# A 16-head attention stage: where TensorE waits for a free PSUM bank, and in which order the next trip's rows are measured

## The chip, the cores and the metric

The kernel runs on one NeuronCore of a Trainium2 chip. The metric is the device time of one execution in microseconds (us); of the kernel before there are three timed runs. Five engines work side by side, each in its own program order, and tell each other of finished work by counting semaphores: TensorE (PE in the profile, its weight loads are PEld), VectorE (DVE), ScalarE (ACT), GpSimd (POOL) and SyncE (SP, which here only starts DMAs). Products of TensorE land in PSUM, which has eight banks of 128 rows by 512 fp32 numbers.

## The reference, cut to what matters

The program is a chain of four residual blocks on an activation of 8 x 512 x 256 in fp32: an attention with one head of 256, a mixture of eight experts, a causal attention with 16 heads, and two layers of local attention. The change lies in the third:

```python
B, T, D, H = (2, 512, 256, 16)        # b is 8 at run time
DH = D // H                            # 16
qkv = x @ Wqkv.T                       # x is the layer-normed activation
q, k, v = ...                          # 16 heads of 16, q and k rotated by position
scores = jnp.einsum('bhqd,bhkd->bhqk', q, k) / math.sqrt(DH)
scores = jnp.where(causal, scores, -jnp.inf)
attn = jax.nn.softmax(scores, axis=-1)
out = jnp.einsum('bhqk,bhkd->bhqd', attn, v)
return out.transpose(0, 2, 1, 3).reshape(b, t, d) @ Wo.T
```

## The kernel before

The third block is the function `phase_attn1`. A barrier over all engines stands before and behind it. It takes the eight rows of the batch in four trips (`pair` in the code, trips 0 to 3 here) of two rows each (`s` 0 and 1, `NS = 2`). Each engine's program is written out by hand as a fixed list; nothing is planned by a scheduler.

A trip has four parts:

- **Projection.** `project`, `project_v` and `flip_qk` make q, k and v of both rows and lay q and k out with the head's numbers on the partitions.
- **The loop over chunks.** The 16 heads of both rows are worked off in eight chunks of two heads a row. Each chunk has six units `u` and six pieces `j`; piece `j` comes `SCORE_LAG` = 11 units behind unit `u`. At step `u` TensorE issues `scores(u)` (line 1301: queries by keys, for the maxima only), at every sixth step `flip_maxima` (line 1310), then `scores_turned(u - 11)` (line 1327: the scores again, keys by queries, with the maxima subtracted by two extra rows of q), and at every second step one of the three parts of `output` (line 1342: probabilities by v, and the row sums).
- **The end of the trip.** `raw_out` (ACT, line 1221), transposes, the division by the row sums (DVE `outputs`), the output projection and the residual, then the transposes of the next trip's rows.
- **The next trip's rows.** DVE's `first_norm(pair + 1)` stands behind the last `row_max` of the loop; it adds up the rows (`whole_rows`), measures them (`row_measure`, mean and variance) and normalises them (`row_norm`). Between measure and norm stands a power on POOL, `power_first` (line 957), for row 0 and then for row 1.

Who waits for whom in the loop:

- `scores(u)` writes one of four banks for each row. `free_place` (lines 1279 to 1287) waits until the user four places back is done: the maximum that DVE takes of it (`row_max`, line 1114), or ACT's copy of the turned maxima. The turned maxima take one of these places a chunk, behind the scores of its third unit.
- `scores_turned(j)` writes one of three banks. The product for row 0 needs the exponential of piece j-2, row 1, to be done, the one for row 1 the exponential of piece j-1, row 0 (ACT `exps`, line 1217; `m = NS * j + s - 3`). At a chunk's first piece it also waits for `nmax_rows` of both rows (line 1317): the maxima must have come back into q by DMA. Their way is `row_max` (DVE), `split_maxima` (POOL), `flip_maxima` (PE), `maxima_out` (ACT, line 1209), four DMAs by SP (line 939).
- Both functions wait for both rows first and then issue both rows' products. Row 0 and row 1 always take different halves of TensorE's 128 rows (`r = 64 * (h % 2)`, and `head` gives the two rows heads of different parity).
- `output(c, part)` needs the causal cut of the probabilities by POOL (`ban_keys`, line 1006), which needs the exponentials; its first part also needs the bank of the chunk before to be copied out (`raw_ready`). Output (7, 0) stands behind piece 45, (7, 1) behind piece 47, (7, 2) behind the end.
- POOL's list has `power_first(0)` and `power_first(1)` of the next trip, one behind the other, between the cuts of piece 41 and those of piece 43.

## Time and profile before

| | |
|---|---|
| median of three runs | 2533.52 us (2532.68 to 2536.14) |
| the profiled execution | 2531.52 us |
| its span, first to last instruction | 2529.8 us |
| mean granted TensorE clock | 0.939 |
| PE busy | 2267.8 us, 90% |
| DVE busy | 1555.9 us, 62% |
| ACT busy | 1315.7 us, 52% |
| POOL busy | 922.6 us, 36% |

The third block lies between about 600 and 1205 us of the span, so each trip takes about 150 us. "Busy" on PE is from modelled ends of pipelined products. The granted clock is a share of full speed, 2.4 GHz; it has two levels, 1.0 and 0.5 (1.2 GHz). An idle time in brackets is that of the engine just before the row's work, with the work that ended it as far as the semaphores tell. Instructions that only wait are called EVENT_SEMAPHORE; they belong to an engine's sequencer and are not busy time.

### The profile page before, as it was taken

What the parts mean: (1) busy time and instruction counts of PE and PEld (TensorE: products, weight loads), DVE (VectorE), ACT (ScalarE), POOL (GpSimd) and SP (SyncE); (2) the same over time, 40 slices, a digit from 0 to 9 for tenths busy, and PEclk for the clock granted to TensorE, in tenths of its full rate; (3) what the DMA queues carried; (4) which work ended last, traced back from release to release, by engine and by line L of the source; (5) the groups of instructions that cost most, each with busy time, mean ns of one, the idle gap of its engine ahead of it and who ended that gap; (6) DMA issues with size and microseconds to landing.
All of it is one profiled execution on the core that took longest, in us unless ns stands there. A gap on an engine that the chain in (4) does not pass through costs nothing.

```text
span 2529.8 us, 45343 instructions
## 1 busy us (share of the span) xinstructions
PE 2267.8 (90%) x15874; PEld 1748.3 (69%) x15874; DVE 1555.9 (62%) x4796; ACT 1315.7 (52%) x3214; POOL 922.6 (36%) x1363
## 2 busy tenths in 40 slices
PE   7999599996778788877699999999999999999998
PEld 5777499994445363544567777777777777777777
DVE  6665422224666757565667676777777667776675
ACT  2221133333555755465555675666755675656753
POOL 2221122213434433332543344333544445343451
PEclk9999699998787988878899999999999999999999
DMA  3222411112001010100200000000101000000000
GB/s 132 100 100 90 130 36 37 39 30 79 19 10 59 3 59 11 35 35 11 88 9 18 16 3 18 18 18 10 44 26 62 19 9 26 26 26 18 10 18 26
DMA packets 75937, 96.41 MB, mean 38 GB/s; under 512 B 6113, under 2 KB 69090, under 8 KB 75458
## 3 DMA queue, kind: packets, MB, share of 16 engines
q1 hardware_dynamic: 70786, 81.89, 9.7%
q0 software_dynamic: 3408, 9.31, 1.3%
q8 instruction: 131, 2.15, 0.4%
q10 hardware_dynamic: 1520, 2.31, 0.3%
q14 instruction: 92, 0.75, 0.1%
HBM read 62.69 MB, written 30.28 MB: 37 GB/s over the span
## 4 chain that ended last, share of the span: by engine, by line
PE 27%; DVE 9%; ACT 8%; issue 5%; POOL 3%; DMA 0%; SPq 0%; DVEq 0%; POOLq 0%; ACTq 0%
PE l_free L2194 4%; PE l_free L2196 4%; PE l_free L2195 3%; PE l_out L2309 3%; PE l_score L2269 2%; POOL l_probs L1684 2%; PE l_turned L2290 2%; DVE l_probsT L1779 2%; DVE l_work L1856 2%; PE l_turned L2194 1%; PE l_turned L2196 1%; PE l_turned L2195 1%; DVE l_u_low L1862 1%; ACT l_probs L2068 1%; PE l_turned L2243 1%
## 5 line engine op out<-in xcount | busy, mean ns | idle before, releaser
L1684 POOL TENSOR_SCALAR l_probs<-l_probs,l_rinv 128x256 f32<-128x256 f32 (+1 forms) x512 | 223.5, 456 | 227.6 <-DVE l_rinv L1839 227.5
L1114 DVE CUSTOM_DVE_ANT_0 c_raw<-cbank,c_later 128x256 f32<-128x256 f32 (+3 forms) x512 | 218.3, 487 | 73.3 <-PE cbank L1301 73.0
L2068 ACT ACTIVATE l_probs<-l_probs,l_nmax 128x256 f32<-128x256 f32 (+1 forms) x512 | 239.9, 473 | 26.5 <-DVE l_nmax L1834 26.4
L1217 ACT ACTIVATE c_cprobsT<-cbank 128x384 f32<-128x384 f32 (+1 forms) x384 | 180.9, 525 | 95.8 <-PE cbank L1327 95.7
L1834 DVE CUSTOM_DVE_ANT_0 l_probs<-l_score,mask,l_inv 128x256 f32<-128x256 f32 (+1 forms) x512 | 200.0, 447 | 28.8 <-PE l_score L2269 28.1
L2194 PE MATMUL l_free<-l_part,l_w_high 128*128 128x512 f32 x384 | 166.4, 433 | 9.6 <-DVE l_probsT L1779 6.6
L2194 PE MATMUL l_free<-l_wqkv_high,l_yT 128*128 128x512 f32 x384 | 159.0, 414 | 1.9 <-DVE l_part L1758 1.9
L1817 DVE COPY l_probsT<-l_turned 128x512 f32<-128x512 f32 (+1 forms) x128 | 79.9, 624 | 131.3 <-PE l_turned L2290 80.3
L1006 POOL TENSOR_SCALAR_AFFINE_SELECT c_cprobsT<-c_cprobsT 128x256 f32<-128x256 f32 x256 | 99.6, 413 | 154.3 <-ACT c_cprobsT L1217 152.2
L2196 PE MATMUL l_free<-l_part,l_w_low 128*128 128x512 f32 x384 | 153.0, 398 | 0.0
L2195 PE MATMUL l_free<-l_yT,l_w_high 128*128 128x512 f32 x384 | 152.8, 398 | 0.0
L2195 PE MATMUL l_free<-l_wqkv_low,l_yT 128*128 128x512 f32 x384 | 152.2, 396 | 0.0
L2196 PE MATMUL l_free<-l_wqkv_high,l_part 128*128 128x512 f32 x384 | 152.0, 396 | 0.0
L760 PE MATMUL h_bank<-m_xsT,m_w1s 128*128 128x128 f32 x1248 | 148.3, 278 | 0.4 <-issue 0.4
L760 PEld LDWEIGHTS h_bank<-m_xsT,m_w1s 128*128 128x128 f32 x1248 | 145.0, 195 | 0.8 <-issue 0.7
L685 POOL DMA_INDIRECT m_xs<-xn_d,source x39 | 62.8, 1610 | 218.4 <-PE xT_bank L748 182.9
L2269 PE MATMUL l_score<-l_kT,l_flipped 64*128 64x256 f32 (+1 forms) x1024 | 129.5, 371 | 13.3 <-DVE l_nmax L1834 13.3
L769 PE MATMUL y_bank<-w,m_hT 128*128 x624 | 141.0, 379 | 0.0
L704 DVE TENSOR_TENSOR m_y<-y_bank,b 128x256 f32<-128x256 f32 x39 | 16.6, 425 | 200.0 <-PE y_bank L769 200.0
L2309 PE MATMUL l_out<-l_probsT,l_v 128*64 128x128 f32 x1792 | 128.1, 283 | 12.6 <-ACT l_oT L2086 12.6
L1327 PE MATMUL cbank<-c_cqT,c_ckT 64*128 64x256 f32 (+2 forms) x512 | 96.4, 409 | 46.8 <-ACT c_cprobsT L1217 39.6
L735 ACT ACTIVATE m_hT<-h_bank,m_b1s 128x128 f32<-128x128 f32 x312 | 89.2, 368 | 84.7 <-PE h_bank L760 75.8
(282 smaller groups left out, 5932.1 us busy)
## 6 DMA issues: line engine op xcount, KB each, us to landing
w<-in_W1T SPq DMA_DIRECT2D x8, 1024.0 KB, 8.0
w<-in_W2T SPq DMA_DIRECT2D x8, 1024.0 KB, 11.8
ys_d<-m_y SPq DMA_DIRECT2D x39, 128.0 KB, 1.7
xn_d<-a_prods SPq DMA_DIRECT2D x8, 512.0 KB, 3.6
c_came<-x_d SPq DMA_DIRECT2D x8, 512.0 KB, 4.9
y_d<-c_raw SPq DMA_DIRECT2D x8, 512.0 KB, 3.7
early_rows<-y_d SPq DMA_DIRECT2D x8, 512.0 KB, 3.7
l_came<-y_d SPq DMA_DIRECT2D x8, 512.0 KB, 3.9
```

Source lines behind the costliest of these rows:

```text
L760: last = pe.matmul(h_bank[2 * (j % 2) + h][:, f, :], w1s[j % 2][:, c, (4 * h + f) * P:(4 * h + f + 1) * P], xsT[:, j % 2, c, :], start=c = ...
L769: last = pe.matmul(y_bank[j % 2][:, 0:D], hT[:, j % 2, f, :], w, start=f == 0, stop=f == FC - 1)
L1114: last = dve.tensor_tensor_reduce(raw[:, CHUNKS - NS + s, h * 2 * P:h * 2 * P + wide], score_place("scores", u, s)[:, h * 2 * P:h * 2 * P ...
L1217: act.activation(probsT[s][:, c % 2, i, k0:k0 + w], turned_place(j, s)[:, 0:w], ACT.Exp).then_inc(probs_ready[s], 1)
L1684: pool.tensor_scalar(a, a, rinv[:, j, r, h:h + 1], 1.0, ALU.mult, ALU.mult).then_inc(normed, 1)
L1834: dve.tensor_tensor_reduce(probs[:, j % 2, r, h, 0:width], score_bank[r][:, 2 * P * h:2 * P * h + width], ban, inv[s][:, w, head:head + 1] ...
L2068: act.activation(a, a, ACT.Exp, bias=nmax[:, j, r, h:h + 1], scale=-1.0, accum_out=rsum[:, j % 2, r, h:h + 1])\
L2194: pe.matmul(out, a[0], b[0], start=start, stop=False)
L2195: pe.matmul(out, a[0], b[1], start=False, stop=False)
L2196: return pe.matmul(out, a[1], b[0], start=False, stop=stop)
L2269: last = pe.matmul(score_bank[half][:, 2 * P * h:2 * P * h + width * P], qT[s][r, p, w * P:(w + 1) * P], kT[s][r, p, k0 * P:(k0 + width) * ...
L2309: last = pe.matmul(out_bank[DH2 * half:DH2 * (half + 1), at:at + P], v[s][:, k0 + k, head:head + DH2], probsT[:, j % 2, half, 2 * h + k, : ...
```

## The change

Four edits in `phase_attn1`:

- In `first_norm`, for trips 1 to 3, `row_measure(1)` is issued before `row_norm(0)`. For trip 0 the order stays.
- In `scores`, the wait for a free place is issued for each row just ahead of that row's first product, no longer for both rows ahead of both. The waits of the first unit (`u == 0`) stay ahead of both.
- In `scores_turned`, the wait for the free bank is moved in the same way. The waits for `nmax_rows` stay ahead of both.
- In the loop over steps, output (7, 0), the first part of the last chunk's outputs, is issued behind piece 46 in place of piece 45.

```diff
-                        row_norm(0)
-                        row_measure(1)
+                        if trip:
+                            row_measure(1)
+                            row_norm(0)
+                        else:
+                            row_norm(0)
+                            row_measure(1)
                         row_norm(1)
...
-                        for s in range(NS):
-                            if u == 0:
+                        if u == 0:
+                            for s in range(NS):
                                 pe.wait_ge(qkT_ready[s], pair * (4 * NT) + 4 * NT)
                                 pe.wait_ge(v_ready[s], pair * NT + NT)
-                            free_place("scores", u, s)
                         wide = max(2, qt + 1) * P
                         for i in range(n):
                             for s in range(NS):
+                                if i == 0:
+                                    free_place("scores", u, s)
...
-                        for s in range(NS):
-                            if j % PER_CHUNK == 0:
+                        if j % PER_CHUNK == 0:
+                            for s in range(NS):
                                 pe.wait_ge(nmax_rows[c % 2][s], pair * (16 * CHUNKS) + 32 * (c // 2 + 1))
-                            m = NS * j + s - 3
-                            if m >= 0:
-                                pe.wait_ge(probs_ready[m % NS], pair * UNITS + m // NS + 1)
                         for kt in kts:
...
                             for s in range(NS):
+                                m = NS * j + s - 3
+                                if kt == kts[0] and m >= 0:
+                                    pe.wait_ge(probs_ready[m % NS], pair * UNITS + m // NS + 1)
...
                         for part in range(3):
-                            if j >= 3 and (j - 3 - 2 * part) % PER_CHUNK == 0 and 0 <= j - 3 - 2 * part < UNITS:
+                            if part == 0 and u == UNITS + SCORE_LAG - 3:
+                                continue
+                            if part == 0 and u == UNITS + SCORE_LAG - 2:
+                                output(CHUNKS - 1, part)
+                            elif j >= 3 and (j - 3 - 2 * part) % PER_CHUNK == 0 and 0 <= j - 3 - 2 * part < UNITS:
                                 output((j - 3 - 2 * part) // PER_CHUNK, part)
```

## Rows read from the trace of the kernel before

**Rows 1.** TensorE's timeline, a chunk of trip 3: start us, length, what [idle before].

```profile
1148.55 0.42 PE L1310 MATMUL cbank<-c_identr,c_nmax_hl 128*32 128x128 f32 x4 [0.44 <-DVE c_cnmax L1114]
...
1153.35 0.49 PE L1327 MATMUL cbank<-c_cqT,c_ckT 64*128 64x512 f32 x2
...
1154.60 0.51 PE L1327 MATMUL cbank<-c_cqT,c_ckT 64*128 64x512 f32 x2 [0.52 <-ACT c_cprobsT L1217]
...
1155.82 0.51 PE L1301 MATMUL cbank<-c_ckT,c_cqT 64*128 64x512 f32 x2
...
1157.11 0.30 PE L1310 MATMUL cbank<-c_identr,c_nmax_hl 128*32 128x128 f32 x2 [0.43 <-DVE c_cnmax L1114]
```

**Rows 2.** Timelines of SP, ACT and DVE in the same chunk.

```profile
1149.61 2.38 SPq L939 DMA_DIRECT2D c_cqT<-c_nmaxT  x4
...
1153.85 1.08 ACT L1217 ACTIVATE c_cprobsT<-cbank 128x512 f32<-128x512 f32 x2 [0.86 <-PE cbank L1327]
...
1156.35 0.69 DVE L1114 CUSTOM_DVE_ANT_0 c_raw<-cbank,c_later 128x512 f32<-128x512 f32 x1 [0.83 <-PE cbank L1301]
```

**Rows 3.** Single lines: instructions, duration ns min/median/max, first and last start; whole trace, then windows.

```profile
L1320 PEldq EVENT_SEMAPHORE  x184: 51/51/51, 666.4 to 1177.8; - x184
...
L1336 PEldq EVENT_SEMAPHORE  x28: 51/51/3101, 677.6 to 1174.0; - x28
...
L1317 PEldq EVENT_SEMAPHORE  x1: 51/51/51, 1153.1 to 1153.1; - x1
...
L1320 PEldq EVENT_SEMAPHORE  x1: 51/51/51, 1154.5 to 1154.5; - x1
...
L1327 PE MATMUL cbank<-c_cqT,c_ckT x2: 473/488/502, 1154.6 to 1154.6; 64*128 64x512 f32 x2
```

**Rows 4.** Timelines of ACT and TensorE in trip 1's first chunk with pieces.

```profile
814.43 1.09 ACT L1217 ACTIVATE c_cprobsT<-cbank 128x512 f32<-128x512 f32 x2 [0.39 <-PE cbank L1327]
...
815.17 0.69 PE L1327 MATMUL cbank<-c_cqT,c_ckT 64*128 64x384 f32 x2 [0.35 <-ACT c_cprobsT L1217]
```

**Rows 5.** POOL's timeline at the end of trip 1's loop.

```profile
873.51 1.05 POOL L957 TENSOR_TENSOR c_crstd<-c_cve,minus_half 128x4 f32<-128x4 f32 x1
878.00 1.01 POOL L957 TENSOR_TENSOR c_crstd<-c_cve,minus_half 128x4 f32<-128x4 f32 x1 [3.44 <-DVE c_cve L71]
878.98 1.64 POOL L1006 TENSOR_SCALAR_AFFINE_SELECT c_cprobsT<-c_cprobsT 128x256 f32<-128x256 f32 x4
```

**Rows 6.** TensorE's timeline there.

```profile
877.63 0.69 PE L1327 MATMUL cbank<-c_cqT,c_ckT 64*128 64x384 f32 x2 [0.67 <-ACT c_cprobsT L1217]
879.90 1.94 PE L1342 MATMUL cbank<-c_cprobsT,c_cv 128*32 128x512 f32 x8 [1.57 <-POOL c_cprobsT L1006]
881.76 0.80 PE L1327 MATMUL cbank<-c_cqT,c_ckT 64*128 64x256 f32 x4
883.23 0.80 PE L1327 MATMUL cbank<-c_cqT,c_ckT 64*128 64x256 f32 x4 [0.67 <-ACT c_cprobsT L1217]
883.95 1.51 PE L1342 MATMUL cbank<-c_cprobsT,c_cv 128*32 128x384 f32 x8
```

**Rows 7.** ACT's timeline there.

```profile
877.00 0.87 ACT L1217 ACTIVATE c_cprobsT<-cbank 128x384 f32<-128x384 f32 x2
878.33 0.87 ACT L1217 ACTIVATE c_cprobsT<-cbank 128x384 f32<-128x384 f32 x2 [0.46 <-PE cbank L1327]
```

**Rows 8.** TensorE's timelines: output (7, 0) of trips 0 and 2, pieces of trip 3.

```profile
731.72 1.93 PE L1342 MATMUL cbank<-c_cprobsT,c_cv 128*32 128x512 f32 x8 [2.73 <-POOL c_cprobsT L1006]
...
1029.37 1.93 PE L1342 MATMUL cbank<-c_cprobsT,c_cv 128*32 128x512 f32 x8 [1.74 <-POOL c_cprobsT L1006]
...
1174.00 0.69 PE L1327 MATMUL cbank<-c_cqT,c_ckT 64*128 64x384 f32 x2 [0.92 <-ACT c_cprobsT L1217]
...
1177.95 0.80 PE L1327 MATMUL cbank<-c_cqT,c_ckT 64*128 64x256 f32 x4 [0.67 <-ACT c_cprobsT L1217]
```

**Rows 9.** Busy us (instructions) of PE, PEld, DVE, ACT, POOL; granted clock, DMA share, GB/s.

```profile
876.00:889.00 13.00, 8.62 (x55) 3.31 (x48) 3.57 (x13) 4.68 (x10) 4.10 (x9) 0.50 0.00 0
```

## The prediction
> **What bounds the kernel now.** I read the timeline of TensorE in the chunk loop first, then those of the engines that end its waits, then the end of a trip. Only `phase_attn1` is touched, and barriers enclose it, so a microsecond saved on its path is one saved in the end.
>
> In the steady loop a chunk takes 8.56 us, from one `flip_maxima` (1148.55) to the next (1157.11) [rows 1]; the trace has five such periods in each of the four trips, 8.53 to 8.57. No engine is full there. One chain closes on itself. The flip at 1148.55 feeds ACT's copy and SP's four DMAs, which begin at 1149.61 [rows 2]. TensorE's sequencer gets past the wait for the landed maxima at 1153.1 [rows 3] and issues the first piece at 1153.35 [rows 1]. ACT begins its exponential at 1153.85, after 0.86 idle [rows 2]; the next piece waits for it, with 0.52 of idle before 1154.60. Then stand an output part and the scores at 1155.82 [rows 1]. DVE has been idle 0.83 when it takes their maximum at 1156.35 [rows 2], and the next flip waits 0.43 for that [rows 1]. Every link waits for the one before it or stands right behind it on TensorE, so what shortens a link shortens the period.
>
> At the end of a trip the chain is another. POOL does the power for row 0 at 873.51, then sits 3.44 until DVE has normalised row 0 and measured row 1, does the second power at 878.00, and only at 878.98 comes to the causal cut [rows 5]. Output (7, 0) needs that cut: TensorE stands 1.57 before 879.90 [rows 6]. Piece 46 is behind it in TensorE's order, though its bank has long been free. The same stall is 2.73 in trip 0 and 1.74 in trip 2; trip 3 has no next trip, and there output (7, 0) did not wait for the cut [rows 8].
>
> **Edit 1, both waits moved to their products.** It removes no wait, but it changes what each wait holds and how it is issued.
>
> How it is issued: a TensorE instruction carries one wait in the trace, further ones are instructions of the sequencer. There are 184 at line 1320 [rows 3] and 156 at line 1285. Output part 0 of chunks 1 to 7 has three waits in the code and one such instruction each, 28 in all [rows 3], so two waits fit into one. After the edit row 0's load carries row 0's wait and row 1's load row 1's, and nearly all of the 340 go. The price of one on the path: it starts at 1154.5 and the product at 1154.60 [rows 3, 1], so at most 0.10, of which 0.051 is its own length. I take 0.08. The steady chain has two. The first stands before 1154.60. The other is at a chunk's first piece, where four waits (two landed maxima, two banks) now take two instructions between 1153.1 and 1153.35 [rows 3, 1], and the three left ahead of row 0's product take one. That makes 0.16, bounds 0.05 to 0.20 a chunk. Five periods by four trips by 0.16 is **3.2 us**.
>
> What it holds: the two rows' products of a piece run at the same time. The pair at 1154.60 is over in 0.51 and each single product lasts 0.473 to 0.502 [rows 3, 1]. So row 0's product alone, put into idle time, takes nothing off TensorE's work behind the wait: row 1's still needs a whole pass. It helps ACT, which gets row 0 before it has run dry. In the steady chunk that is worth nothing, since the chain there goes through row 1's product. It does help where pieces follow each other closely at the slow clock. In trip 1's first chunk with pieces ACT idled 0.39 before 814.43, and piece 2 started at 815.17 only after that exponential (0.35 idle) [rows 4]. With row 0 in time, ACT starts 0.39 earlier and the piece goes as soon as TensorE is through with the scores before it. The piece's own idle bounds this at 0.35. I add 0.1 for the waits of the two pieces after it and 0.1 for the second product ahead of the first flip: 0.55 for the start of a trip, bounds 0.1 and 0.8. Four trips: **2.2 us**. Between the last flip and the end of the loop the saved instructions of three more pieces count, 0.2 a trip: **0.8 us**.
>
> Where TensorE has a backlog, the sequencer is ahead of it and the waits are hidden in both versions: zero. Every product starts at the earliest when its own conditions hold and no later than before, and the consumers' orders are fixed, so I see no place where the waiting itself makes anything later.
>
> The Trainium skill (Perfetto Trace Analysis, Identifying Dependency Chains) says that an instruction with more waits may get EventSemaphore instructions ahead of it; the trace agrees with its 184 and 156. The page gives no price. At zero a piece the term of 3.2 would be nothing, and that result is the first rival.
>
> **Edits 2 and 3, the end of a trip.** With `row_measure(1)` ahead of `row_norm(0)`, DVE has both variances before POOL comes to the powers at 873.51: DVE has then been idle since it added row 1 up, over 3 us, and a norm and a measure together fit into POOL's 3.44. So the powers follow each other, 873.51 to about 875.6 [rows 5], and the cut of piece 43 waits for its exponential alone, which is over before ACT begins piece 44's at 877.00 [rows 7]. Two cuts of 0.41 (a quarter of 1.64 [rows 5]) are done by 877.8, before TensorE, at piece 45 from 877.63 on, reaches output (7, 0) in either place. Cost: row 0's norm comes no later, since it waits for the power, and row 1's comes earlier.
>
> What is late next, in the order of edit 3: piece 45 at 877.63, its exponential from 878.33, 0.44 for row 0 (half of 0.87) [rows 7], so piece 46 at 878.8 in place of 881.76. Behind it output (7, 0): piece 47 was followed by its output after 0.72 (883.23 to 883.95), and output (7, 0) was followed by the next piece after 1.86 [rows 6]. Piece 47 then goes at 878.8 + 0.72 + 1.86 = 881.4 in place of 883.23: **1.8 us** in trip 1. From piece 47 on (its exponentials, the cut of the last keys, output (7, 2), the copy) the chain is as before. Edit 1 adds here: ACT idles 0.46 before 878.33 with row 0's bank free [rows 7], so up to 0.5 more; I take 0.4, so 2.2. The 1.8 is the stall of 1.57 and 0.25; with its stall of 1.74 trip 2 gives 2.0 + 0.4 = 2.4. Trip 0, with 2.73, gives 3.0, and up to 0.9 more (half of 1.86) if output (7, 0), which ran at the slow clock there (1.93) [rows 8], now falls into the fast one; I take 3.8 in all. In trip 3 there was no stall. Piece 47 still stands behind output (7, 0): 1174.00 + 0.70 (877.63 to 878.33) + 0.44 + 0.72 + 1.86 = 1177.7 for 1177.95 [rows 8], 0.2, and 0.3 for ACT. Together 2.2 + 2.4 + 3.8 + 0.5 = **8.9 us**, bounds 7.0 (no help from edit 1) and 10.5.
>
> Edit 3 alone is worth little beside edit 2: whichever of piece 46 and output (7, 0) goes first, piece 47 waits for both, and the gain is the wait for one exponential hidden under the output, 0.3 a trip; it is in the sums above. Without edit 2 it would let piece 46 go under the stall.
>
> **Sum.** 3.2 + 2.2 + 0.8 + 8.9 = 15.1 us. The profiled execution took 2531.5 us with its 1.7 around the span, so it would take 2516.4. The median of the runs lies 2.0 above it: **2518.4 us**.
>
> The granted clock is the part that I can't work out. The end of trip 1's loop ran at 0.50, 1.2 GHz, throughout, though PE was busy for 8.62 of 13.00 us there [rows 9]; output (7, 0) took 1.94 in it [rows 6]. Moved work meets the change of level elsewhere. If one such output a trip changes level either way, 0.9 each, that is 3 to 4 us over the kernel; I put 3 us on both sides for it.
>
> **Rivals.**
> 1. *The waits' instructions cost nothing.* A wait carried by a load could take as long to be seen as one of its own, or the chain could go by the path over the fifth piece's output and not over the DMAs. For it: the profile calls the idle before a load "issue" rather than a wait. Against: the product follows that instruction by 0.10 each time. Then 3.2 and most of 0.8 and 2.2 are missing, 9 to 10 us remain: 2524.
> 2. *The end's gain is given back.* POOL's stall goes but the clock takes it: a wrong phase at four trips' ends, or piece 47 behind output (7, 0) at the slow clock in trip 0. Then the loop's 6 us and some 2 to 3 of the end remain: 2525.
> 3. *Pairs come apart.* With a wait between them, row 1's product could start late even where both banks are free, and a pair would take two passes. For it: the two now start together, behind all waits. Against: the sequencer is ahead wherever TensorE has work waiting. It costs a pair between nothing and the 0.50 that a product lasts. There are 384 pairs with a moved wait (12 a chunk), so it decides from 15.1 / 384 = 0.04 us on each; at 0.06, about what one sequencer's instruction takes, it costs 23 us: 2541, slower.
> 4. *No change.* All that is saved is met by the clock: 2533.
>
> The Trainium skill (TensorE: Matmul & The Clock Gate, Part 3) has matmuls on different row groups run at once but start and end in program order. By it a late row 1 also holds what stands behind it. The trace agrees with the overlap, 0.51 for two; what a wait between the two does, no row shows.
>
> **How the numbers follow.** Forecast 2518.4 with 0.64 (its own range 2513 to 2524), rival 1 with 0.17, rival 2 with 0.10, rival 3 with 0.05, rival 4 with 0.04. The range is 2511 to 2527: below by the upper bounds of the terms (19) and 3 of clock, above over rivals 1 and 2. About 0.2% (5 us) is what a measurement of this kernel tells from no change. Faster by more: 0.91; within: 0.05; slower by more: 0.04.
>
> **What would show it.** Steps at lines 1285 and 1320 all but gone from the sequencer's instructions; steady periods of 8.35 to 8.45 us between flips; POOL's two powers within 2.1 us; output (7, 0) without a wait for POOL, behind piece 46; the last output part 2 to 4 us nearer to piece 45 in trips 0 to 2. Wrong would be: periods of 8.55 as before (rival 1), pairs that start more than 0.05 apart where TensorE has no idle (rival 3), a longer time at 0.50 (rivals 2 and 4).

## The result

2501.98 us in the median (2500.28 to 2507.50, four runs) against 2533.93 for the kernel before on the same chip; the ratio is 0.9874, 95% interval 0.9857 to 0.9891. That is 32 us gained where 15.1 were forecast, and below the range. The two profiled executions lie 24.0 us of span apart (2529.8 to 2505.8); the profiled one was the slowest of the four, with 0.944 for the mean granted clock against 0.950 and 0.951 in the other three.

### The profile page after: what moved, and what is told of

It reads as the page before. It is cut to its first block, busy times and chain, and to the rows that moved or that the text cites. A ratio compares the mean times of both kernels' runs of the same rounds, so it can differ in the third digit from the quotient of the medians.

```text
span 2505.8 us, 44975 instructions
## 1 busy us (share of the span) xinstructions
PE 2285.2 (91%) x15874; PEld 1764.6 (70%) x15874; DVE 1553.9 (62%) x4796; ACT 1313.2 (52%) x3214; POOL 921.1 (37%) x1363
## 4 chain that ended last, share of the span: by engine, by line
PE 27%; DVE 9%; ACT 8%; issue 5%; POOL 3%; DMA 0%; SPq 0%; DVEq 0%; POOLq 0%; ACTq 0%
PE l_free L2203 4%; PE l_free L2205 4%; PE l_free L2204 3%; PE l_out L2318 3%; PE l_score L2278 2%; POOL l_probs L1693 2%; PE l_turned L2299 2%; DVE l_probsT L1788 2%; DVE l_work L1865 2%; PE l_turned L2203 1%; PE l_turned L2205 1%; PE l_turned L2204 1%; DVE l_u_low L1871 1%; ACT l_probs L2077 1%; PE l_turned L2252 1%
## 5 line engine op out<-in xcount | busy, mean ns | idle before, releaser
L1332 PE MATMUL cbank<-c_cqT,c_ckT 64*128 64x256 f32 (+2 forms) x512 | 117.0, 396 | 25.8 <-ACT c_cprobsT L1221 16.5
```

## The profile after

TensorE's timeline of the chunk in trip 3 that answers to [rows 1]. The piece behind the first, `x2` at 1154.60 before, is now one product for row 0 at 1123.94 and one for row 1 at 1124.55:

```profile
1118.75 0.42 PE L1315 MATMUL cbank<-c_identr,c_nmax_hl 128*32 128x128 f32 x4 [0.43 <-DVE c_cnmax L1118]
...
1123.40 0.50 PE L1332 MATMUL cbank<-c_cqT,c_ckT 64*128 64x512 f32 x2
...
1123.94 0.39 PE L1332 MATMUL cbank<-c_cqT,c_ckT 64*128 64x512 f32 x1
1124.55 0.50 PE L1332 MATMUL cbank<-c_cqT,c_ckT 64*128 64x512 f32 x1 [0.22 <-ACT c_cprobsT L1221]
...
1125.77 0.50 PE L1306 MATMUL cbank<-c_ckT,c_cqT 64*128 64x512 f32 x2
...
1127.06 0.41 PE L1315 MATMUL cbank<-c_identr,c_nmax_hl 128*32 128x128 f32 x4 [0.43 <-DVE c_cnmax L1118]
```

From flip to flip it is 8.31, before 8.56. The first piece stands 4.65 behind its flip (before 4.80), the next 1.15 behind it (before 1.25), and from there on every distance is as it was.

The sequencer's instructions that carry a wait, by line; count, duration min/median/max in ns:

```profile
L1329 PEldq EVENT_SEMAPHORE  x28: 51/1248/1512, 675.2 to 1146.3; - x28
L1339 PEldq EVENT_SEMAPHORE  x68: 51/51/51, 670.1 to 1158.7; - x68
L1341 PEldq EVENT_SEMAPHORE  x28: 51/51/51, 680.0 to 1153.3; - x28
```

Those for the turned scores' banks fell from 184 [rows 3] to 28, one at a chunk's first piece, where the landed maxima are waited for as well; in `scores` 156 went and none is left. Those of the outputs (L1341 is L1336 of before) stayed at 28.

The end of trip 1's loop on POOL and on TensorE, for [rows 5, 6]:

```profile
866.55 2.18 POOL L957 TENSOR_TENSOR c_crstd<-c_cve,minus_half 128x4 f32<-128x4 f32 x2
868.58 0.81 POOL L1006 TENSOR_SCALAR_AFFINE_SELECT c_cprobsT<-c_cprobsT 128x256 f32<-128x256 f32 x2
```

```profile
868.42 0.87 PE L1332 MATMUL cbank<-c_cqT,c_ckT 64*128 64x384 f32 x3
869.59 1.56 PE L1332 MATMUL cbank<-c_cqT,c_ckT 64*128 64x384 f32 x5 [0.30 <-ACT c_cprobsT L1221]
871.08 1.93 PE L1347 MATMUL cbank<-c_cprobsT,c_cv 128*32 128x512 f32 x8
872.94 0.80 PE L1332 MATMUL cbank<-c_cqT,c_ckT 64*128 64x256 f32 x4
873.67 1.51 PE L1347 MATMUL cbank<-c_cprobsT,c_cv 128*32 128x384 f32 x8
875.96 1.51 PE L1347 MATMUL cbank<-c_cprobsT,c_cv 128*32 128x256 f32 x16 [0.78 <-POOL c_cprobsT L1006]
```

The two powers follow each other without the 3.44 between them, the cut comes right behind them, and output (7, 0) at 871.08 waits for nobody, behind piece 46. The steps that were forecast happened. But compare the four ends. Windows from the last flip to the last output part, trips 0 to 3; columns: length, busy us of PE, PEld, DVE, ACT, POOL, the granted clock, DMA:

```profile
720.40:734.10 13.70, 10.21 (x84) 4.21 (x83) 7.43 (x26) 10.00 (x23) 8.36 (x18) 1.00 0.01 2
860.90:876.00 15.10, 12.45 (x84) 4.94 (x85) 7.35 (x26) 10.03 (x23) 8.29 (x18) 0.76 0.01 2
1003.60:1017.30 13.70, 10.22 (x84) 4.22 (x84) 7.39 (x26) 9.98 (x23) 8.29 (x18) 1.00 0.01 2
1142.70:1158.90 16.20, 13.59 (x84) 5.35 (x85) 0.00 (x0) 10.25 (x23) 5.71 (x15) 0.68 0.01 2
```

The same 84 products take 13.7 us where the clock was 1.00 throughout and 15.1 or 16.2 where it had a part at 0.50. In the kernel before none of the four ends kept its fast clock.

To place the gain I cut every profiled execution at the same instructions, and added up its four trips. *Start* is from the first scores to the third flip, *chunks* from there to the eighth and last flip, *tail* from there to the last output part, *end* from there to the first `wo` product, *half* the time of the tail at a granted clock of 0.50. Us:

```
kernel                                          start  chunks    tail     end    half
before                                          114.0   167.3    72.5    44.6    39.1
changed, first profile                          108.7   162.2    58.4    43.0    17.3
changed, again (all_again)                      107.4   162.2    54.5    43.2     0.0
edit 1 (waits_only)                             109.1   162.3    68.0    45.2    22.2
its half at first scores (waits_scores)         113.5   167.3    73.3    44.4    43.5
its half at turned scores (waits_turned)        107.4   162.3    70.7    44.3    37.1
edit 2 (measure_only)                           113.2   167.3    68.4    44.4    43.1
edit 3 (output_only)                            115.7   167.4    69.0    41.2    37.2
edits 2, 3 (tails_only)                         118.6   167.3    68.4    38.9    41.3
edits 1, 3 (waits_output)                       109.2   162.2    65.9    43.7    25.0
edits 1, 2 (no_output)                          109.2   162.3    57.5    45.0    11.5
one wait, row 0 held (one_wait_held)            112.7   162.4    69.9    44.2    23.1
row 0 free, both waits (row0_free_two_waits)    113.2   163.5    69.0    44.9    24.0
one wait held, edits 2, 3 (held_tails)          113.0   162.4    61.1    43.0    20.9
edit 2, added products (measure_fill)           116.5   167.2    61.1    39.0     0.0
all, added in the tail (all_fill_tail)          108.5   162.3    58.2    40.0     0.0
all, added at the start (all_fill_start)        107.7   162.2    60.3    44.6    28.9
all, and trip 0's order (all_trip0)             110.6   162.2    61.3    45.7    28.2
```

The first two rows give 5.3 + 5.1 + 14.1 + 1.6 = 26.1 us. Outside the cuts the profiled execution lost some 2: the untouched stretch ahead of the loop was 3.8 us longer. The second profile gives 6.6 + 5.1 + 18.0 + 1.4 = 31.1 us. Its 2499.46 us and granted clock of 0.950 are those of most timed executions, so it is the better guide.

## The experiments

Ratios are to the kernel before on the same chip, with 95% intervals; gains in us are (1 - ratio) times 2533. The intervals reach 2.4 to 4.7 us to each side.

**The three edits one by one, and together again.** Each kernel is the one before with only the named hunks of the diff.

`waits_only`, edit 1:

```diff
-                            free_place("scores", u, s)
+                                if i == 0:
+                                    free_place("scores", u, s)
...
+                                if kt == kts[0] and m >= 0:
+                                    pe.wait_ge(probs_ready[m % NS], pair * UNITS + m // NS + 1)
```

> The change's first edit alone: each wait at its product, the tails as before. The changed kernel gained 32 us where 15.1 were forecast. Theory A (the waits were mis-sized): in the trace of the changed kernel the steady period fell by 0.25 us in place of 0.16, and the stretch from the first scores to the third flip by 1.36, 0.66, 1.49 and 1.80 us; four steady periods by four trips, one shorter period by four, and those starts make 4.0 + 1.1 + 5.3 = 10.4 us, and a microsecond or two at the ends: 2521 to 2524. Theory B (the forecast's size, and the excess lies in the ends): 6.2 us, 2527 to 2528. Periods of 8.28 to 8.32 under A; 8.35 to 8.45 under B.

0.9949 (0.9935 to 0.9963), 12.9 us; periods of 8.28 to 8.33. Theory A, with more than its 10.4.

`measure_only`, edit 2:

```diff
-                        row_norm(0)
-                        row_measure(1)
+                            row_measure(1)
+                            row_norm(0)
```

> The second edit alone: on later trips both rows are measured before row 0 is normalised. Theory A (the tails add up as the forecast's steps say, with the third edit worth 0.3 a trip): 6 to 9 us, 2525 to 2528; POOL's two powers within 2.2 us, output (7, 0) without a wait for the causal cut in trips 0 to 2, trip 3 unchanged. Theory B (the clock is the larger part: a shorter stall keeps TensorE at the fast level at the trip's end): 12 us and more, below 2522, with the stretch at 0.50 behind the last flip of trips 0 and 2 cut from 13.7 and 17.1 us to some 3.

0.9974 (0.9964 to 0.9984), 6.6 us, with the tail at 17.10 or 17.11 in all four trips. Theory A by size; and the clock did not stay up: 43.1 us at half speed. Trip 3, which was to stay unchanged, took 0.9 us more (17.11 for 16.20), with 10.8 us at 0.50 for 6.9.

`output_only`, edit 3:

```diff
+                            if part == 0 and u == UNITS + SCORE_LAG - 3:
+                                continue
+                            if part == 0 and u == UNITS + SCORE_LAG - 2:
+                                output(CHUNKS - 1, part)
```

> The third edit alone: output (7, 0) one piece later, DVE's order as before. Piece 46 can go under POOL's stall of 3.44 us, but the output still waits for the cut and piece 47 stands behind it. Theory A (as forecast): piece 46 no longer stands behind the output, and one exponential (0.44) is hidden in each trip, up to the 0.7 that the piece takes: 1 to 3 us, 2530 to 2533, within measurement of no change. Theory B (the order is a large part of the gain, since ACT gets piece 46 2 to 3 us earlier and the tail of the pipeline follows it): 5 us and more, 2528 or less.

0.9975 (0.9966 to 0.9985), 6.3 us: theory B. Alone it was worth as much as the reordered measuring.

`all_again`, the changed kernel unchanged:

> The changed kernel once more, beside its parts on the same chip: 2500 to 2504. If the three parts alone sum to 28 to 36 us they are independent; if they sum to under 24, one of the edits only pays beside another (theory B of the others: the third edit beside the second, or the clock, which stays up only when both stalls are gone).

0.9870 (0.9854 to 0.9886), 32.9 us. The parts sum to 25.8, which lies between the two limits that were set (28 and 24). Some 7 us belong to no edit alone, but the four intervals together (the root of their squares' sum, 6.4 us) are nearly as large. The pairs below are clearer: edit 1 alone and the other two together give 12.9 + 9.1 = 22.0, so 10.9 are missing there.

**The pairs, and edit 1 by halves.** `no_output` has edits 1 and 2, `tails_only` 2 and 3, `waits_output` 1 and 3, `waits_turned` edit 1 in `scores_turned` alone; each is the sum of hunks shown above.

> The first and second edits together, output (7, 0) in its old place. Alone they took 12.9 and 6.6 us off (ratios 0.9949 and 0.9974), the third alone 6.3, all three 33. Theory A (the first two add, and the third is worth its 6 us anywhere, since it puts piece 46 ahead of a long output part): 2533 - 19.5 = 2514. Theory B (the surplus of 7 us lies between the waits and the measuring): 2507 or less. Theory C (the surplus needs the third edit: only with piece 46 early does TensorE stay busy enough to keep its fast clock to the last output): 2514 or more, with 13 us and more at 0.50 behind the last flip of each trip, against 3.4 in the kernel with all three.

0.9906 (0.9892 to 0.9919), 23.8 us: more than A's 19.5, at the edge of B. Two of its four tails ran at full clock, and two had 5.7 us at half speed, less than C wanted.

> The second and third edits together, the waits as before. Theory A (additive): 2533 - 12.9 = 2520. The forecast's own number for the two was 8.9 with 1.3 of it from the first edit: 2525 to 2526. Theory C (the fast clock held at the end is the surplus and the two edits suffice for it): 2514 to 2516, with the last output part 13.6 to 14.5 us behind the last flip in all four trips and 3.4 us at 0.50 there.

0.9964 (0.9949 to 0.9979), 9.1 us. The forecast had 7.0 to 8.9 for the two, without and with edit 1's help, and the time came near it; theory A's 12.9 is the very edge of the interval. Its twelve executions, us and mean granted clock of each:

```
2513.58 0.948   2516.18 0.947   2519.16 0.945   2521.79 0.946
2525.98 0.941   2526.71 0.938   2526.93 0.937   2527.62 0.939
2527.75 0.938   2528.46 0.938   2529.99 0.938   2531.68 0.938
```

One program, 18 us apart, and the order is nearly that of the clock. The two shortest lie where theory C had all of them. The profiled execution (2527.62) was of the longer kind, so where the clock stayed up in the short ones no profile shows; and 9.1 is a mean over both kinds.

> The first and third edits together, DVE's order as before: POOL's stall of 3.4 us stays in trips 0 to 2. Theory A (additive): 2533 - 19.2 = 2514. Theory C: the stall before output (7, 0) is still there, so the clock falls there in trips 0 to 2 and the surplus is missing or shows in trip 3 alone: 2514 to 2518. If instead the time is near 2507, the surplus lies between these two edits and not with the measuring.

0.9929 (0.9916 to 0.9941), 18.0 us: here the two add.

> The first edit in the turned scores alone (their bank waits at their products); the first scores wait as before, for both rows ahead of both. The edit in both places took 12.9 us off. In the steady chunk the trace has 0.13 us saved ahead of the chunk's first piece and 0.09 ahead of the next one, both turned scores. Theory A (all of the gain is in the turned scores, the other 156 instructions stand where TensorE has a backlog): 2520 to 2522, steady periods 8.28 to 8.34. Theory B (both halves count, the scores' at the start of a trip where row 0's bank is free before row 1's): 2523 to 2527, with the stretch from the first scores to the first flip as in the kernel before and only the steady part shortened.

0.9947 (0.9935 to 0.9959), 13.4 us: theory A, all of edit 1's gain.

**The instruction or the freedom of row 0.** Row 0 is called free where its product may go before row 1's bank is. `one_wait_held` keeps both rows behind one wait, for the exponential that ends later:

```diff
-                            m = NS * j + s - 3
-                            if m >= 0:
-                                pe.wait_ge(probs_ready[m % NS], pair * UNITS + m // NS + 1)
+                        m = NS * j - 2
+                        if m >= 0:
+                            pe.wait_ge(probs_ready[m % NS], pair * UNITS + m // NS + 1)
```

> The kernel before, with one wait ahead of both rows of a turned piece in place of two: that for the younger exponential, which ACT does after the older one, so nothing is waited for less. It takes the extra instruction away and still holds row 0. The first edit in the turned scores took 13.4 us off. Theory A (the instruction is the price: 0.08 to 0.13 us on each of two links a chunk): the steady period falls from 8.55 to some 8.35 and the ends too; 2520 to 2526. Theory B (what counts is that row 0 is free to go, so that ACT always has a row ready and never idles between exponentials): little, 2529 to 2533, periods of 8.45 and more, and ACT still idles 0.15 to 0.5 us before each piece's exponentials behind the last flip.

0.9951 (0.9937 to 0.9966), 12.4 us. Its chunk on TensorE, and `row0_free_two_waits` below it, whose edit is

```diff
+                                for m in range(NS * j - 3, NS * j + s - 2):
+                                    if kt == kts[0] and m >= 0:
+                                        pe.wait_ge(probs_ready[m % NS], pair * UNITS + m // NS + 1)
```

> The kernel before, with row 0's wait at its product and, ahead of row 1's product, both waits once more: row 0 is free to go, and the extra instruction of the sequencer stays, now ahead of row 1. Theory A (the instruction is the price): 2529 to 2533, periods of 8.5 and more. Theory B (row 0's freedom is the price): most of the 13.4 us, 2520 to 2524, ACT without idle between the exponentials behind the last flip; the steady period keeps part of the gain, 8.35 to 8.45, since the link through row 1 still has the instruction.

0.9956 (0.9942 to 0.9970), 11.1 us. TensorE's timeline in the first kernel, from the chunk's first piece to the next flip, and then the same in the second:

```profile
1150.10 0.50 PE L1327 MATMUL cbank<-c_cqT,c_ckT 64*128 64x512 f32 x2
...
1151.25 0.50 PE L1327 MATMUL cbank<-c_cqT,c_ckT 64*128 64x512 f32 x2 [0.42 <-ACT c_cprobsT L1217]
...
1153.76 0.42 PE L1310 MATMUL cbank<-c_identr,c_nmax_hl 128*32 128x128 f32 x4 [0.43 <-DVE c_cnmax L1114]
```

```profile
1149.57 0.60 PE L1327 MATMUL cbank<-c_cqT,c_ckT 64*128 64x512 f32 x2
...
1150.82 0.47 PE L1327 MATMUL cbank<-c_cqT,c_ckT 64*128 64x512 f32 x1 [0.29 <-ACT c_cprobsT L1217]
...
1153.29 0.42 PE L1310 MATMUL cbank<-c_identr,c_nmax_hl 128*32 128x128 f32 x4 [0.44 <-DVE c_cnmax L1114]
```

Their sequencers' instructions at the turned scores, the first kernel and the second:

```profile
L1320 PEldq EVENT_SEMAPHORE  x28: 51/547/787, 676.2 to 1165.6; - x28
```

```profile
L1324 PEldq EVENT_SEMAPHORE  x212: 51/51/1446, 667.3 to 1172.0; - x106
```

By time and period each kernel met the theory that it was meant to favour: the first kernel theory A, and the second theory B (periods of 8.34 to 8.39). The links say why. In the steady chunk theory A holds: with the instruction gone and row 0 held, the chunks take 162.4 us, those of the changed kernel 162.2. The second kernel tells the links apart. Ahead of the chunk's first piece it has one instruction fewer before row 0's product, and saves as much there (the flip was at 1144.92, so 4.65 behind it, for 4.80 before); ahead of the next piece the kept instruction stands before row 1's product, and that piece is 1.25 behind the first, as before, where the first kernel has 1.15. Its period is 8.35, between 8.55 and 8.30. Row 0's freedom adds nothing there.

At a trip's start it is otherwise: neither kernel alone shortens the sum much (112.7 and 113.2 for 114.0), and the half of edit 1 that does both brings it to 107.4. The sum hides what row 0's freedom does. From the first flip to the second, where ACT takes the first pieces, trips 1 to 3 took 8.86 to 8.89 before, 8.76 to 8.79 with row 0 held, 8.32 to 8.35 with row 0 free and the instruction kept, and 8.25 to 8.30 with both, so nearly all of it is the freedom. The first interval went the other way (10.1 us in three trips of each of these two kernels, 10.0 and 10.1 in two of the kernel before, 9.72 else and in `waits_turned`), and the third goes mostly by the clock, as shown below. And a good part of the 11 to 12 us of these two is clock: 23 and 24 us at half speed in the tail for 39, with trip 3's tail at 14.2 and 14.0 us for 16.2.

**What lies behind the last flip.** `held_tails` has edits 2 and 3 and the one held wait:

> The second and third edits with the single wait held ahead of both turned rows (the extra instruction gone, row 0 not free). With the full first edit the three took 33 us off; the second and third alone 9. The single held wait alone took 12.4 us. Theory A (the saved instruction gives the surplus, wherever it stands): as with all three, 2500 to 2504, the last output part 13.6 to 15.1 us behind the last flip. Theory B (behind the last flip it is row 0's freedom that keeps ACT, and through it TensorE, busy): the sum of the parts, 2510 to 2516, with the last part 16 to 17 us behind the flip and ACT idle 0.1 to 0.5 ahead of each piece's exponentials.

0.9939 (0.9925 to 0.9953), 15.5 us, less than the sum of its parts (21.5) and 17 short of the changed kernel. That refutes theory A. It is nearer to theory B, though both missed: its tails are 14.7 and 15.9 us, not 16 to 17, and the time lies just above B's. Against the second profile of the changed kernel 5.6 us of the shortfall are at the starts and 6.6 in the tails, where 20.9 us ran at half speed for none. ACT's timelines show what row 0's freedom does there. `measure_only` (both rows held, extra instruction), then `held_tails`, then the changed kernel again, each from the exponentials of piece 42 on; trip 3, trip 1 and trip 1:

```profile
1166.05 1.09 ACT L1221 ACTIVATE c_cprobsT<-cbank 128x512 f32<-128x512 f32 x2 [1.00 <-PE cbank L1331]
1167.59 1.08 ACT L1221 ACTIVATE c_cprobsT<-cbank 128x512 f32<-128x512 f32 x2 [0.46 <-PE cbank L1331]
1169.09 0.60 ACT L1225 ACTIVATE c_raw<-cbank 128x512 f32<-128x512 f32 x1 [0.41 <-PE cbank L1346]
1169.68 0.87 ACT L1221 ACTIVATE c_cprobsT<-cbank 128x384 f32<-128x384 f32 x2
1171.00 0.87 ACT L1221 ACTIVATE c_cprobsT<-cbank 128x384 f32<-128x384 f32 x2 [0.46 <-PE cbank L1331]
```

```profile
869.68 2.27 ACT L1221 ACTIVATE c_cprobsT<-cbank 128x512 f32<-128x512 f32 x4 [1.00 <-PE cbank L1331]
871.85 0.60 ACT L1225 ACTIVATE c_raw<-cbank 128x512 f32<-128x512 f32 x1
872.32 1.91 ACT L1221 ACTIVATE c_cprobsT<-cbank 128x384 f32<-128x384 f32 x4
874.44 0.87 ACT L1221 ACTIVATE c_cprobsT<-cbank 128x384 f32<-128x384 f32 x2 [0.21 <-PE cbank L1331]
```

```profile
860.33 2.06 ACT L1221 ACTIVATE c_cprobsT<-cbank 128x512 f32<-128x512 f32 x4 [1.14 <-PE cbank L1332]
862.33 0.60 ACT L1225 ACTIVATE c_raw<-cbank 128x512 f32<-128x512 f32 x1
862.83 2.60 ACT L1221 ACTIVATE c_cprobsT<-cbank 128x384 f32<-128x384 f32 x6
```

With row 0 free, ACT runs eleven instructions in 5.10 us without a pause (860.33 to 865.43). With both rows held they take 5.63, with pauses of 0.1 inside the runs and 0.21 at the end. In `measure_only` nine of them take 5.82, but from 1166.4 on at the slow clock; the other two ran wholly at the fast one. Row 0's product runs under the previous exponential, so ACT's chain no longer passes through a load and a product at every piece. In the tail no scores stand between, and ACT is what the pieces wait for. Trip 3 gives the price at equal clock, as three kernels without edits 2 and 3 ran its tail wholly at 1.00: 14.17 us with row 0 held (`one_wait_held`), 13.97 with row 0 free and the instruction kept (`row0_free_two_waits`), 13.76 with edit 1. Row 0's freedom is worth 0.4 us a trip beside the saved instruction. The rest of the shortfall in the tails has the form of the clock.

`waits_scores` is edit 1 in `scores` alone:

> The first edit in the first scores alone. In both places it took 12.9 us, in the turned scores alone 13.4. Theory A (the scores' waits stand where TensorE has a backlog, or where DVE's maximum sets the pace): 2531 to 2535, no change; steady periods 8.53 to 8.57. Theory B (row 0's scores early feed DVE at the start of a trip): the first flip 0.4 us nearer to the first scores in each trip, 1 to 2 us in all, 2530 to 2533.

1.0005 (0.9993 to 1.0017), no change: theory A. The first flip did come 0.4 to 0.7 us earlier in each trip (9.36 behind the first scores for 9.72 to 10.06), 2.0 us in all. In the profile the third intervals took 1.6 of it back, trip 0's with 11.46 us for 10.04, where the clock was back at 1.00 later.

**The clock.** `measure_fill` adds work to `measure_only`:

```diff
+                        if u >= UNITS + MAX_LAG - 1 and j < UNITS - 1:
...
+                            spare = score_bank[(rotation.index(("maxima", CHUNKS - 1, 0)) + 1) % 4]
+                            for _ in range(1):
+                                pe.matmul(spare[:], kT[0][:, 0, 0:P], qT[0][:, 0, :], start=True, stop=True)
```

> The kernel with the second edit alone, whose last output part stood 17.1 us behind the last flip in all four trips with 17.1 us of TensorE at 0.50 there, and with one idle-time product of 512 columns into an unused scores bank after each of the last nine pieces' output slots, whose result nobody reads. It adds work of about 0.43 us each. Theory A (the clock is the cause of the long tail): TensorE keeps its fast clock behind the last flip, and the tail falls to 14 to 15 us in spite of the added work: 8 to 12 us less than 2525.7, 2514 to 2518. Theory B (the tail is 17.1 us because of its chain through ACT and POOL, the clock follows from it): no gain, the added work costs 0 to 2 us a trip, 2526 to 2533.

0.9923 (0.9910 to 0.9937), 19.5 us: theory A, 12.9 us better than the kernel that it adds work to. By the profiles the tails fell by 7.3 us and the ends by 5.4, and the starts took 3.3 more. The tail of trip 3 without the products and with them:

```profile
1160.10:1177.30 17.20, 12.52 (x84) 4.63 (x86) 0.00 (x0) 10.43 (x24) 5.77 (x16) 0.68 0.01 2
```

```profile
1155.30:1170.60 15.30, 12.27 (x92) 5.08 (x94) 0.00 (x0) 10.26 (x23) 5.75 (x15) 1.00 0.00 1
```

Eight products more, 1.8 us less, and a granted clock of 1.00 (2.4 GHz) for 0.68, a mixture of that and 0.50 (1.2 GHz). TensorE had stood idle 0.6 to 0.75 us before most pieces, and with the products at most 0.35 was left. The Trainium skill (TensorE: Matmul & The Clock Gate, Part 1, HAM oscillation) tells of this gate falling while matmuls wait for a DMA and of the price that the next ones pay. The price is in this trace, with 17.2 and 15.3 us; the waits are others, mostly for ACT, and no idle time in the 10 us ahead of the fall was longer than 0.75.

`all_fill_tail` does the same to the changed kernel (that hunk in all three edits), `all_fill_start` fills idle time ahead of the first scores:

```diff
+                            n_fill = {(8, 1): 3, (9, 1): 3}.get((i, j), 0)
+                            if n_fill:
+                                pe.wait_ge(v_ready[0], pair * NT + NT)
+                            for _ in range(n_fill):
+                                pe.matmul(bank[0][1][:], xnT[0][:, 0, 0:P], xnT[0][:, 0, :], start=True, stop=True)
...
+                    for _ in range(1):
+                        pe.matmul(bank[0][1][:], xnT[0][:, 0, 0:P], xnT[0][:, 0, :], start=True, stop=True)
```

> The changed kernel with one idle-time product of 512 columns after each of the last nine pieces' slots, read by nobody, as the kernel with the second edit and such products, where the tail fell from 17.1 to 15.3 us and the time by 9 to 13 us. Theory A (the surplus of the changed kernel is this same clock, already held): little is left, 0 to 3 us either way, 2498 to 2503, the tail between 13.6 and 14.5 us in every trip and no trip at 15.1. Theory B (the clock still falls in many timed executions and the products hold it): 2492 to 2497. Theory C (the added products now stand in the way, since TensorE has less idle time there): 2504 to 2510.

0.9876 (0.9858 to 0.9894), 31.4 us: theory A. Where the clock is held already, the products cost 0.9 a tail (14.54 for 13.62), 3.7 in all. In the profile the ends behind them were 3.2 shorter, and in time nothing is gained.

> The changed kernel with all three edits, and seven idle-time products of 512 columns (0.485 us each by the projections' rows) where TensorE waits for the last flips of q and k: three, three and one, of 1.45, 1.67 and 0.89 us idle; nobody reads them. TensorE's clock falls there at each trip's start and stays at 0.50 for 24 to 27 us, in which the first 14 us of scores keep it busy. Theory A (the idle stretches bring the clock down, and the scores behind them are bound by it): 2 to 5 us less a trip, 2480 to 2492. Theory B (the clock falls anyway, or the scores there are bound by DVE's maxima, not by TensorE): 2500 as before, or up to 4 us more for the added work.

0.9898 (0.9882 to 0.9914), 25.8 us: 7 less than the changed kernel. Theory A is refuted, and the loss is larger than theory B's 4. The clock did fall later at the start (17.1 us at 0.50 for 23.9 and more), and the first flip came 0.3 nearer (9.06 to 9.10 for 9.36). But the first scores came 1.2 to 1.5 us later. The clock was back at 1.00 only 3.2 to 3.4 us behind the second flip, for 2.4 to 2.6 in the second profile of the changed kernel, and the third interval took 9.5 or 9.6 for 9.1 or 9.2. So the start took 107.7 for 107.4: an early stretch at the fast clock is worth 0.3 us there, and a late one is worth more. And the same instructions in the tail now met the slow clock, in all four trips. Trip 0's tail here, and that of the changed kernel:

```profile
720.40:735.50 15.10, 12.51 (x84) 5.00 (x86) 7.30 (x26) 10.00 (x23) 8.23 (x18) 0.76 0.01 2
```

```profile
714.70:728.40 13.70, 10.21 (x84) 4.25 (x86) 7.39 (x26) 9.97 (x23) 8.34 (x18) 1.00 0.01 2
```

`all_trip0` drops the `if trip:` and measures both rows first everywhere:

```diff
-                        if trip:
-                            row_measure(1)
-                            row_norm(0)
-                        else:
-                            row_norm(0)
-                            row_measure(1)
+                        row_measure(1)
+                        row_norm(0)
```

> The changed kernel with the measuring of both rows first on the first trip as well, for a version that may be faster. The first trip's rows are normalised before the chunk loop. Theory A (nobody waits there for the first row alone): 2500 to 2503, no change. Theory B (TensorE's first transposes of row 0 wait for that norm, which now comes one measuring later): 0.5 to 2 us more.

0.9906 (0.9888 to 0.9925), 23.8 us, 9 worse than the changed kernel: both theories missed. In its profile all four tails have a stretch at 0.50 (15.07, 16.10, 15.07 and 15.07 us), the last of them some 500 us behind the edit, and its five timed executions have a mean clock of 0.939 to 0.946. The loss has the form of the clock; why the slow stretches came to lie so is open. No version tried beats the changed kernel.

## Why the prediction was wrong in size

The step that failed is the clock: it was set down as 3 us of noise on both sides, beside terms that hold at one clock. The runs show it as the largest part of what is missing behind the last flip (18.0 us for 9.7), and as a part at the starts. The saved instruction and the freed row were the right causes, and their sizes were too small.

**Edit 1 in the steady chunks: right cause, price too small.** 3.2 us forecast, 5.1 measured (167.3 to 162.2). I had 0.08 us for each of two links; they measured 0.15 and 0.10, so the sum of 0.25 lies above my upper bound of 0.20. In the trace of before, the sequencer's instructions in a row start 0.11 apart, twice their own length of 0.051, and 0.08 was too near to the length. The count was nearly right: four periods of 8.53 to 8.57 fell by 0.25, and the fifth, which I had wrongly put in the same band, is 7.64 and fell by 0.27. That nearly all of the 340 instructions go (312 did) and that row 0 early is worth nothing there held; `one_wait_held` shows the second.

**Pairs did come apart.** Counted in the traces, none of the 512 pairs of `scores` and `scores_turned` products starts more than 0.05 us apart before, and 164 do in the changed kernel's first profile. At 99 of them TensorE had no idle time just before either product: the sign that was set down for rival 3. The two rows' products then run one behind the other. From the second scores of trip 0 on, the kernel before and then `waits_scores`:

```profile
650.82 0.69 PE L1301 MATMUL cbank<-c_ckT,c_cqT 64*128 64x384 f32 x2 [1.04 <-DVE c_cnmax L1114]
```

```profile
650.24 7.88 PE L1302 MATMUL cbank<-c_ckT,c_cqT 64*128 64x384 f32 x18 [0.33 <-DVE c_cnmax L1114]
```

Before, these 18 products stand with idle time between them and end 10.03 us behind the first scores; run without a pause, with the rows one behind the other, they end 9.43 behind them. Over the four trips TensorE is busy for 145.4 us of the chunks where it was for 140.3, and for 97.1 of the starts for 82.8, and yet the time fell: the places waited for are not free earlier, and row 0 uses the time until row 1's is. Whether a busier TensorE also has a part in which clock the tails get, no run separates. `one_wait_held`, in which no pair comes apart, kept the fast clock in one tail of four, as `waits_only` did.

**Edit 1 at a trip's start: mis-sized, and in part the clock.** 2.2 us forecast, 5.3 to 6.6 measured. I had taken the gain of one piece (0.35) and 0.1 for two more. But ACT's pauses went at every piece: in trip 1 of the changed kernel's second profile the first six exponentials are one run,

```profile
802.39 2.84 ACT L1221 ACTIVATE c_cprobsT<-cbank 128x512 f32<-128x512 f32 x6 [4.46 <-PE cbank L1332]
```

where before the second pair alone had 0.39 ahead of it [rows 4]. The first two intervals, both wholly at the slow clock, fell by 0.4 and 0.6 us in that trip (9.73 to 9.36, 8.86 to 8.26), the third by another 0.4. Over the four trips the three intervals give 2.0, 2.4 and 2.2 us in the second profile. The first of these, by `waits_scores`, brought nothing when it came alone. The third is not edit 1's alone. Over all the kernels it goes from 8.44 us, where the clock was back at 1.00 0.4 us behind the second flip (`waits_turned`, trip 1), to 11.46, where that was 8.5 us behind (`tails_only`, three trips). Where the clock is back at the same moment, edit 1 takes 0.1 to 0.2 off it: 9.33 to 9.13 at 2.4 us, 10.04 to 9.86 at 4.15. So some 1.5 us of the surplus at the starts are the clock's, an estimate from these rows.

**Behind the last flip: the step that failed.** For the end of the loop I had 0.8 for edit 1's instructions and 8.9 for edits 2 and 3 with its help, 9.7; the tails fell by 14.1 us in the first profile and 18.0 in the second. The ends, at which I had put nothing, gave 1.6 and 1.4 more. By trips, against the first profile: 2.4 forecast for trip 1, which kept a slow stretch, and 3.7 measured; 4.0 and 2.6 for trips 0 and 2, which ran wholly at the fast clock, and 5.1 each; 0.7 for trip 3, and 0.1, with 10.2 us at half speed for 6.9 before. So where only the kernel before had a slow stretch the gain was 1.1 and 2.5 us more than forecast. Where both had one, it was 1.3 more with that stretch shortened by 5.4 us (trip 1) and 0.6 less with it lengthened by 3.3 (trip 3). How much the whole of edit 1 is worth at equal clock no pair of runs shows cleanly, since no tail of the kernel before was wholly fast. An estimate: `measure_fill`, wholly at the fast clock, has tails of 15.3, its products cost 0.9 a tail where the clock was up anyway, and `no_output` has 13.75, so 0.6 or 0.7 a trip, about what was forecast. Yet timed, edit 1 took 17.2 us beside edit 2 (6.6 to 23.8) and 12.9 alone. I had priced it as time on a path. What it also does is keep ACT, and so TensorE, from pausing just where the clock is about to fall.

**Edits 2 and 3.** Between 7.0 and 8.9 us by themselves; 9.1 (5.3 to 12.9) measured. The steps for DVE, POOL and the order of TensorE were seen, but that the sum came out so near is luck. In the profile of `tails_only` the tails fell by 4.1 us, the ends, which I had at nothing, by 5.7, and the starts took 4.6 more: ends of 9.2 us at a clock of 1.00, and starts with the clock back late. Edit 3 beside edit 2 was put at 0.3 a trip. At equal clock it is 0.13 in tails wholly at 1.00 (13.75 to 13.62) and nothing in those with a stretch at 0.50 (15.0, 15.07), so the order itself is worth no more than I said; yet timed it took 9 us off (23.8 to 32.9). The profiles of `no_output` and `all_again` lie 7.2 us apart: 3.0 in the tails, of which four of four kept the fast clock for two of four, and 1.8 each at the starts and ends.

**The clock: 3 us on both sides was far too narrow, and not symmetric.** The part of the tails at half speed went from 39.1 us to 17.3 and, in the second profile, to none, and the tails from 72.5 to 58.4 and 54.5. A tail costs 1.4 us more with 7.2 us at 0.50 and 2.5 more with 10.2. I had treated the clock as noise that meets moved work; but an edit that takes idle time out of TensorE also decides which clock the rest gets. This is where most of the 7 us lie which no edit has alone: the tails fall by 4.5, 4.1 and 3.5 us in the three single kernels and by 18.0 in the kernel with all. Why a given trip falls on one side is not settled. In the two tails of the changed kernel's first profile in which it fell, it did so 8 and 6 us behind the last flip, behind the same instructions as in the two in which it did not.

**The rivals.** Rival 1 is refuted by `one_wait_held`. Rival 3's sign was seen and its price was not: the periods fell and `waits_turned` gained 13.4 us. Something like rival 2, a gain at the end given back by the clock, shows in `tails_only`, without edit 1: where the end of a trip was 2 us shorter (9.2 for 11.2) the next start was 1.8 us longer (30.1 for 28.3), with 34.1 us at 0.50 for 27.3. That the one brought the other is not shown: trip 0's start, with no such end before it, took 30.15 us too.

## What to carry to other kernels

Where two consumers share one producer, put each wait at the instruction that needs it: the price of holding the first back is paid at every round in which the consumer runs dry, so count the rounds and don't price one. Free the instruction too: a wait that a load can carry costs about 0.1 us less on the path than one that needs an instruction of its own. And when an edit takes idle time out of TensorE, read the granted clock behind it, trip by trip; forecast with both levels and a chance for each, as the tail here takes 13.6, 15.1 or 16.1 us with the same instructions.

## What the runs showed of the hardware

Work that nobody reads made a kernel 12.9 us faster (0.9974 to 0.9923), with no part of its tails at 0.50 for 43.1 us; added where the clock was already up it cost 0.9 us a trip, and added somewhere else it made the kernel 7 us slower, with a slow stretch in all four tails. The clock fell behind idle times of at most 0.75 us (`measure_only`). How late it comes back decides an interval of a start, 8.44 to 11.46 us. One program on one core can be 18 us apart from run to run (2513.58 to 2531.68), with a granted clock of 0.948 and 0.938. And of two waits at one load, the extra instruction could hold the one that came last: before the change, it is that instruction at 1154.49 which stands behind the exponential's end at 1154.45, and the product starts 0.14 behind that end; in the changed kernel, where the load carries the wait, it is 0.05.
